# Moving the weight transposes of values and output out of the preamble of a fused attention and expert layer

## The chip, the cores and the metric

The kernel runs on one core of a Trainium2 chip. The metric is the device time of one execution in microseconds; where a kernel was run several times, the median. The engines are named as in the profile: PE (TensorE), DVE (VectorE), ACT (ScalarE), POOL (GpSimd), SP (SyncE, which here issues nearly all DMAs).

## The reference, cut to what matters

Eight batches of 512 tokens with 512 features pass a gated cross attention with 16 heads, then a mixture of 8 experts. The edit touches only the attention's beginning.

```python
def proj(x, W, b):
    return (x @ W.T + b).reshape(B, S, H, Hd).transpose(0, 2, 1, 3)
Q, K, V = proj(query, Wq, bq), proj(key, Wk, bk), proj(value, Wv, bv)   # query = layernorm(x); key = value = ctx
scores = jnp.einsum('bhqd,bhkd->bhqk', Q, K) / SCALE
attn = jax.nn.softmax(scores, axis=-1)
out = jnp.einsum('bhqk,bhkd->bhqd', attn, V)
out = out.transpose(0, 2, 1, 3).reshape(B, S, D)
x = x + jnp.tanh(g_xattn[0]) * (out @ Wo.T + bo)
x = x + jnp.tanh(g_ffn[0]) * ffn(layernorm(x))     # 8 experts, top 2, capacity limited
```

## The kernel before, in words

Each engine has one instruction list, written out by hand, and waits on semaphores. Every projection is a product of numbers split into a high and a low f16 part (three matmuls for each of four blocks of 128 features, so 12 matmuls of 128x512 a projection tile).

**Preamble.** The four weight matrices `Wq, Wk, Wv, Wo` (numbered n = 0 to 3) and the two inputs of batch 0 (`xn`, the normalised x, and `cin`, the context) have to be turned, since the contraction dimension must lie on the partitions. One *tile* is 128 features of one matrix by 512: PE writes it into a PSUM bank with 4 transposes of 128x128 f32 (`transposes`, L1207), ACT copies it out as the f16 high part (`wT[:, n, 0]`, L682, or `actT[:, n, 0]`, L677) and DVE subtracts that from PSUM for the low part (`wT[:, n, 1]`, L861, or `actT[:, n, 1]`, L853) and frees the bank. The preamble uses the four banks of `RING` (0, 1, 2, 4) in turn, so PE can be at most four tiles ahead of DVE. The order is Wq, `xn`, Wk, `cin`, Wv, Wo: 24 tiles, of which 16 are of weights. `Banks` numbers the uses of each bank; `claim` makes PE wait until all earlier uses of a bank were read, `filled` makes a reader wait for PE, `copied` waits until a use was read.

Ahead of it DVE and POOL do the layer norm of batch 0 (DVE statistics L828 and L831, POOL the inverse deviation L514 and L517, DVE the normalisation L835). PE waits first for `small_in` (biases, gates and the router's weights, six DMAs) and turns the biases; ACT does Tanh and the scaled output bias (L666 to L672) with it. At the end of the preamble DVE sets two rows of `stk` to a constant (L867, `k_ones`), and PE and SP wait until all of Wo's tiles were read.

SP issues the DMAs in this order: x of batch 0, Wq, the small inputs, Wk, context of batch 0, Wv, Wo. They land in buffers that are used for something else later: Wq and Wk in `pt`, Wv in `v32`, Wo in `xres`.

**Batch 0** (and, in a loop, the others). PE computes four of the eight projection tiles of queries and keys (`queries_keys(i)`, L1278, i = 0 to 3: q0, k0, q1, k1) and two of the four of values (`values`, L1325). ACT copies each projection twice (L715, L717), POOL subtracts (L536), SP stores it to DRAM and loads it back in the layout of the heads (`stack_heads`, L367 and L371: `stk<-qk_rows`). Then come 23 *slots*. In slot s PE computes four score blocks (`scores(s, 0..3)`, L1288, banks 0, 1, 0, 1); DVE takes the maximum of each (L874), which frees the bank. Slots 0, 1, 3 and 4 hold a further projection of queries and keys, in two halves (`filling`), slot 2 the router's transposes of `x2n` (banks 6, 7, 3, 5), slot 4 the router's products, slots 5 and 6 the other values. DVE also does one block of the layer norm of the next batch in each of the slots 1 to 4. From slot 6 on the exponentials and from slot 7 on the products with values run beside the scores.

Of the kernel before, what the change touches and what calls it, by code (L numbers as in the profile page):

```python
# [16 lines left out]
P = 128  # L17
KT = D // P
# [27 lines left out]
LN_SLOT = 1  # L46
QK_FIRST, QK_SLOT = 4, (0, 1, 3, 4)
V_FIRST, V_SLOT = 2, (5, 6)
X2T_SLOT, PARTS_SLOT, LG_SLOT = 2, 4, 5
# [11 lines left out]
def later_v(s):  # L61

    return [V_FIRST + j for j, slot in enumerate(V_SLOT) if slot == s]


# [30 lines left out]
def layer_kernel(nc, x, ctx_in, g_x, g_f, Wq, bq, Wk, bk, Wv, bv, Wo, bo, Wr, br, W1, b1, W2, b2, out):  # L96
# [9 lines left out]
    with stack:  # L106
# [113 lines left out]
        def act_banks(n):  # L220
            for kt in range(KT):
                banks.add(("actT", n, kt), RING[kt])

        banks.add("bias", 6)
        for n in range(4):
            for kt in range(KT):
                banks.add(("w", n, kt), RING[kt])
            if n < 2:
                act_banks(n)
        pre = banks.close(1)  # L230
# [160 lines left out]
        def _(sp):  # L391
# [20 lines left out]

            for kt in range(KT):
                copied(sp, pre, ("w", 3, kt))

            def store_rows(b):
# [10 lines left out]
            def batch(b, first, last):  # L427
# [11 lines left out]
                for g in range(NG):  # L439

                    sp.wait_ge(mrow_ready, NG * b + g + 1)
                    rows = stk[96:98, 0, 4 * g:4 * g + 4, :].rearrange("o h (t a q) -> o (h t) a q", t=KT, a=4)
                    for a in range(4):
                        sp.dma_start(rows[:, :, a, :], mrow[32 * a:32 * a + 32, g, :]).then_inc(mrow_in[g], 16)
                    if g == 0:
                        for i in range(QK_FIRST + 2, NQ):
                            stack_heads(sp, b, i)
                    if g == STORE_GROUP:
                        if not first:
                            store_rows(b)  # L450

                            sp.wait_ge(x1_stored, 16 * KT * b)
                            sp.wait_ge(x2n_ready, KT * b)
                        settle(sp)
                        sp.dma_start(xres[:, :, :], x_b[b]).then_inc(xres_in, 16)
# [41 lines left out]
        def _(pool):  # L497
# [165 lines left out]
        def _(act):  # L663
            s = nc.scalar
            act.wait_ge(small_in, 96)
            s.activation(tg[:, 1:2], tg[:, 0:1], ACT.Tanh).then_inc(tanh_done, 1)  # L666
            act.wait_ge(tanh_done, 1)
            s.activation(tg[:, 2:3], tg[:, 1:2], ACT.Copy, scale=1.0 / (SA * SW)).then_inc(tgbo_ready, 1)
            s.activation(tgbo[:, :], tgbo[:, :], ACT.Copy, scale=tg[:, 1:2]).then_inc(tgbo_ready, 1)
            ps, read = filled(act, pre, "bias")  # L670
            s.activation(bias[:, 0:8], ps[:, 0:8], ACT.Copy, scale=SQ).then_inc(bias_ready, 1)
            s.activation(bias[:, 8:12], ps[:, 8:12], ACT.Copy, scale=SA).then_inc(read, 1)  # L672

            def inputs_hi(n, kt):
# [3 lines left out]

            for n in range(4):
                for kt in range(KT):  # L680
                    ps, _ = filled(act, pre, ("w", n, kt))
                    s.activation(wT[:, n, 0, kt, :], ps, ACT.Copy, scale=SW).then_inc(w_hi, 1)  # L682
                if n < 2:
                    for kt in range(KT):
                        inputs_hi(n, kt)
            act.wait_ge(bias_ready, 1)
# [18 lines left out]

            def batch(b, last):
                rows, parts, logits = router_copy(use, b, b)
# [16 lines left out]
                heads_stacked(act, b)  # L724
                for i in range(QK_FIRST):
                    queries_keys(i)
                for tt in range(V_FIRST):
                    values(tt)
                for t in range(SLOTS + 1):
                    for i in later_qk(t):  # L730
                        queries_keys(i)
                    if t == X2T_SLOT:
                        rows()
# [26 lines left out]
                    if t in GROUP_NORM:  # L760
# [3 lines left out]
                                     bias=bias[:, 8 + gr:9 + gr]).then_inc(a_hi, 1)  # L764
            batch(0, False)
            with act.Fori(1, B - 1) as b:
# [54 lines left out]
        def _(dve):  # L821
# [33 lines left out]

            for n in range(4):
                for kt in range(KT):

                    dve.wait_ge(w_hi, KT * n + kt + 1)
                    ps, read = read_by_last(pre, ("w", n, kt))  # L860
                    v.scalar_tensor_tensor(wT[:, n, 1, kt, :], ps, SW, wT[:, n, 0, kt, :],  # L861
                                           ALU.mult, ALU.subtract).then_inc(read, 1)
                if n < 2:
                    for kt in range(KT):
                        inputs_split(0, n, kt)
            dve.wait_ge(tgbo_ready, 2)
            v.memset(stk[96:98, 1, :, :], SQ * SQ).then_inc(k_ones, 1)  # L867

            def batch(b, last):
                def maxima(t, qts):  # L870
# [17 lines left out]
                for t in range(SLOTS + 1):  # L888
                    maxima(t, (0, 1))
                    if t % 4 == 0 and 4 <= t <= UNITS:  # L890
# [51 lines left out]

            batch(0, False)
            with dve.Fori(1, B - 1) as b:
# [251 lines left out]
        def _(pe):  # L1196
# [27 lines left out]

            for n in range(4):
                pe.wait_ge(w_in[n], 16)
                for kt in range(KT):
                    dst, full = claim(pe, pre, ("w", n, kt))
                    transposes(dst, [raw[n][:, m, kt * P:(kt + 1) * P] for m in range(KT)]).then_inc(full, 1)
                if n < 2:  # L1230
                    for kt in range(KT):
                        inputs_transposed(0, n, kt)

            for kt in range(KT):
                copied(pe, pre, ("w", 3, kt))

# [28 lines left out]
            def batch(b, last_batch, first=False):  # L1265
# [290 lines left out]
```

## Time and profile before

| | |
|---|---|
| median of 3 runs | 1928.5 us (1927.63 to 1929.86) |
| the profiled execution's own time | 1927.96 us |
| its span | 1926.2 us |
| PE busy | 1778.0 us, 92% of the span |
| DVE busy | 1156.4 us, 60% |
| ACT busy | 778.9 us, 40% |
| POOL busy | 474.9 us, 25% |
| chain that ended last | PE 82%, DVE 10%, issue 3%, ACT 2% |

The span is the time between the first and the last record of the profile; about 1.8 us of the execution lie around it. Busy time says which engine has most to do over the whole, but the edit concerns the first 62 us alone, so the stretch matters more than the shares. All times in the rows below are microseconds from the span's start; in the timeline a row can hold several instructions ("x4"), its time then reaching from the first one's start to the last one's end, and brackets tell how long the engine was idle before it and what released it.

### The profile page before, as it was taken

How to read it: one execution, taken by the hardware profiler on the slowest of the kernel's cores; microseconds unless marked ns; L12 is line 12 of the kernel's file. 1: busy time of each engine (PE TensorE's matmuls, PEld its weight loads, DVE VectorE, ACT ScalarE, POOL GpSimd, SP SyncE). 2: the span in 40 equal slices, each digit the busy share in tenths (PEclk: the TensorE clock that was granted, in tenths of full speed). 3: DMA queues.
4: the chain of work that ended last, by engine and by line, in shares of the span. 5: the costliest groups of instructions: out<-in, count | busy, mean ns of one | idle time of the engine just before them, and what ended most of it. 6: DMA issues, size and time to landing. Idle time of an engine off the chain costs nothing.

```text
span 1926.2 us, 30517 instructions
## 1 busy us (share of the span) xinstructions
PE 1778.0 (92%) x10822; PEld 921.7 (48%) x10822; DVE 1156.4 (60%) x2163; ACT 778.9 (40%) x1012; POOL 474.9 (25%) x451
## 2 busy tenths in 40 slices
PE   7999999999999999999501999999999999999996
PEld 4334242333424333242200766666676767666664
DVE  5777777777777777867685653535353544534330
ACT  4444635445363544536310534425151615334240
POOL 2322424232242323221232111212212122112101
PEclk9999999999999999999755999999999999999998
DMA  6213232241313314032220242534343342425311
GB/s 222 90 45 110 67 126 93 76 142 44 109 66 117 101 63 135 21 108 69 89 92 27 68 140 50 162 71 136 75 122 102 100 125 74 133 63 147 73 37 25
DMA packets 138206, 178.97 MB, mean 93 GB/s; under 512 B 45493, under 2 KB 86593, under 8 KB 134057
## 3 DMA queue, kind: packets, MB, share of 16 engines
q1 hardware_dynamic: 97192, 157.85, 24.9%
q0 software_dynamic: 40960, 20.41, 6.0%
q8 instruction: 33, 0.54, 0.1%
q14 instruction: 21, 0.16, 0.0%
HBM read 134.08 MB, written 43.63 MB: 92 GB/s over the span
## 4 chain that ended last, share of the span: by engine, by line
PE 82%; DVE 10%; issue 3%; ACT 2%; POOL 1%; DMA 1%; SPq 0%; DVEq 0%; ACTq 0%; POOLq 0%
PE psum L1510 22%; PE psum L1487 20%; PE psum L1307 7%; PE psum L1314 7%; PE psum L1298 6%; PE psum L1288 5%; PE psum L1278 5%; PE psum L1400 4%; PE psum L1325 2%; DVE mx L874 2%; PE psum L1207 2%; ACT osum L759 1%; PE psum L1463 1%; DVE cmp L1024 1%; DVE x2hl L938 1%
## 5 line engine op out<-in xcount | busy, mean ns | idle before, releaser
L1510 PE MATMUL psum<-w,hT 128*123 128x512 f16 x1920 | 420.3, 379 | 0.0
L1487 PE MATMUL psum<-xgT,w 128*128 128x308 f16 (+1 forms) x3072 | 411.3, 294 | 0.6 <-DVE xgT L1133 0.6
L874 DVE TENSOR_REDUCE mx<-psum 128x1 f32<-128x512 f32 x512 | 331.1, 684 | 108.3 <-PE psum L1288 105.9
L1487 PEld LDWEIGHTS psum<-xgT,w 128*128 128x128 f16 x3072 | 298.4, 97 | 109.8 <-DVE xgT L1133 0.8
L1510 PEld LDWEIGHTS psum<-w,hT 128*123 128x123 f16 x1920 | 257.9, 135 | 148.8
L748 ACT ACTIVATE pt<-psum 128x1024 f32<-128x1024 f32 x256 | 259.1, 1021 | 166.4 <-PE psum L1298 165.8
L802 ACT ACTIVATE h<-psum,b1c 128x308 f32<-128x308 f32 (+1 forms) x256 | 117.9, 511 | 382.2 <-PE psum L1487 381.8
L1151 DVE TENSOR_TENSOR hT<-h,hT 128x615 f16<-128x615 f32 x128 | 102.6, 801 | 212.2 <-ACT hT L805 212.2
L651 POOL DMA_INDIRECT out_dram<-y,idx_now x40 | 98.9, 2472 | 499.6 <-DVE y L1186 273.9
L1278 PE MATMUL psum<-actT,wT 128*128 128x512 f16 x768 | 179.2, 381 | 2.0 <-DVE wT L861 2.0
L1288 PE MATMUL psum<-stk 96*128 96x512 f16 x512 | 171.0, 383 | 4.2 <-DVE mx L874 1.7
L786 ACT ACTIVATE w<-stage 128x2048 f16<-128x2048 f32 x64 | 121.6, 1901 | 99.2 <-DMA stage<-in_L_ffn_W_dram 99.2
L1128 DVE SCALAR_TENSOR_TENSOR w<-stage,w 128x512 f16<-128x512 f32 x240 | 156.7, 684 | 0.3 <-issue 0.3
L1298 PE MATMUL psum<-stk 98*128 98x512 f16 x512 | 153.6, 381 | 0.0
L1307 PE MATMUL psum<-pt,v 128*32 128x512 f32 x1024 | 136.4, 604 | 5.3 <-ACT osum L759 5.0
L1314 PE MATMUL psum<-pt,ones 128*32 128x512 f32 x1024 | 136.2, 604 | 0.0
L1183 DVE SCALAR_TENSOR_TENSOR y<-psum,b2b 123x512 f32<-123x512 f32 x40 | 27.7, 692 | 178.8 <-PE psum L1510 178.8
L536 POOL TENSOR_TENSOR qks<-qk,qks 128x512 f16<-128x512 f32 x64 | 75.2, 1175 | 197.4 <-ACT qks L717 143.3
L1288 PEld LDWEIGHTS psum<-stk 96*128 96x128 f16 x512 | 43.7, 98 | 166.8 <-DVE mx L874 122.9
L1278 PEld LDWEIGHTS psum<-actT,wT 128*128 128x128 f16 x768 | 75.1, 98 | 91.0 <-issue 4.4
L605 POOL DMA_INDIRECT xg<-x_split,idx_new x40 | 62.0, 1550 | 222.0 <-issue 179.0
L715 ACT ACTIVATE qk<-psum,bias 128x512 f32<-128x512 f32 x64 | 44.0, 687 | 179.0 <-PE psum L1278 173.8
(181 smaller groups left out, 1644.7 us busy)
## 6 DMA issues: line engine op xcount, KB each, us to landing
stage<-in_L_ffn_W_dram SPq DMA_DIRECT2D x64, 1024.0 KB, 5.1
stk<-qk_rows SPq DMA_DIRECT2D x192, 128.0 KB, 2.5
qk_rows<-qks SPq DMA_DIRECT2D x64, 256.0 KB, 2.5
xin<-in_x_dram SPq DMA_DIRECT2D x8, 1024.0 KB, 5.3
cin<-in_ctx_dram SPq DMA_DIRECT2D x8, 1024.0 KB, 7.5
xres<-in_x_dram SPq DMA_DIRECT2D x8, 1024.0 KB, 5.6
out_dram<-xres SPq DMA_DIRECT2D x32, 256.0 KB, 2.1
x_split<-x2hl SPq DMA_DIRECT2D x32, 256.0 KB, 2.3
```

The source lines that it names most:

```text
L748: s.activation(pt[:, (2 * u + hf) % 4, :, :], psum[:, bank:bank + 2, :], ACT.Exp, scale=1.0 / (math.sqrt(HD) * SQ * SQ)).then_inc(read, 1)
L786: s.activation(dst, stage[:, i % 2, :], ACT.Copy, scale=SW).then_inc(chunk_hi, 1)
L802: s.activation(h32[:, m % 4, c0:c1], psum[:, (2 * m + ch) % 4, 0:c1 - c0], ACT.Silu, scale=1.0 / (SX * SW), bias=b1c[:, e, m:m + 1]).then_ ...
L874: v.reduce_max(mx[:, KT * t + qt:KT * t + qt + 1], ps, AX.X).then_inc(read, 1)
L1128: v.scalar_tensor_tensor(part[1], stage[:, i % 2, cols], SW, part[0], ALU.mult, ALU.subtract).then_inc(chunk_split, 1)
L1278: last = t_.matmul(psum[:, bank, :], wT[:, n, wp, kt, m * P:(m + 1) * P], actT[:, n, xp, kt, :], start=(kt == 0 and (wp, xp) == (0, 0)), s ...
L1288: t_.matmul(dst, stk[0:96, 0, s, qt * P:(qt + 1) * P], stk[0:96, 1, s, :], start=True, stop=True).then_inc(full, 1)
L1298: last = t_.matmul(psum[:, 2 + 2 * hf + j, :], stk[0:98, 1, h, kt * P:(kt + 1) * P], stk[0:98, 0, h, :], start=True, stop=True)
L1307: t_.matmul(psum[32 * j:32 * j + 32, 6, :], v32[:, kt, HD * h:HD * h + HD], pt[:, (2 * u + j // 2) % 4, j % 2, :], start=(kt == 0), stop=( ...
L1314: last = t_.matmul(psum[32 * j:32 * j + 32, 7, :], ones32[:, :], pt[:, (2 * u + j // 2) % 4, j % 2, :], start=(kt == 0), stop=(kt == KT - 1))
L1487: mm = t_.matmul(psum[:, (2 * m + ch) % 4, 0:c1 - c0], w1[:, wp, kt, m * P:(m + 1) * P], xgT[:, xp, kt, c0:c1], start=(kt == 0 and (wp, xp ...
L1510: mm = t_.matmul(psum[0:CP, Y_BANK[c], :], hT[:, hp, k, c * CP:(c + 1) * CP], w2[:, wp, k, :], start=(k == 0 and (hp, wp) == (0, 0)), stop ...
```

## The change

The preamble keeps 16 tiles: Wq and Wk, then `xn` and `cin`. PE starts Wq without `small_in`; the bias transpose stands behind Wk, and ACT's small inputs between `xn`'s and `cin`'s tiles. Wv is turned in batch 0 between projections 1 and 2 (banks 6, 7, 3, 5), Wo in two pairs at the end of slots 0 and 1 (banks 6, 7, 6, 7). PE's wait until a matrix is read stands now ahead of its first use (for Wo ahead of the output projection), SP's wait for Wo's ahead of the load of `xres`. The memset of `stk` goes from DVE to POOL, behind the last inverse deviation of batch 0. The diff, cut to its core:

```diff
+WV_AFTER = 2
+WO_SLOT = (0, 0, 1, 1)
+def wo_tiles(s):
+    return [kt for kt, slot in enumerate(WO_SLOT) if slot == s]
...
-        banks.add("bias", 6)
-        for n in range(4):
+        for n in range(2):
             for kt in range(KT):
                 banks.add(("w", n, kt), RING[kt])
-            if n < 2:
-                act_banks(n)
+        banks.add("bias", 6)
+        for n in range(2):
+            act_banks(n)
+        for n, ring in ((2, (6, 7, 3, 5)), (3, (6, 7, 6, 7))):
+            for kt in range(KT):
+                banks.add(("w", n, kt), ring[kt])
...
 # SP: the wait moves from behind the first loads to the load of xres in batch 0
+                        else:
+                            for kt in range(KT):
+                                copied(sp, pre, ("w", 3, kt))
...
 # POOL, behind the inverse deviations of batch 0
+            pool.wait_ge(ln_rstd[0], KT)
+            g.memset(stk[96:98, 1, :, :], SQ * SQ).then_inc(k_ones, 1)
+            pool.wait_ge(k_ones, 1)
...
 # ACT
+            for n in range(2):
+                for kt in range(KT):
+                    weights_hi(n, kt)
+            for n in range(2):
+                for kt in range(KT):
+                    inputs_hi(n, kt)
+                if n == 0:
+                    small_inputs()
...
                 for i in range(QK_FIRST):
+                    if first and i == WV_AFTER:
+                        for kt in range(KT):
+                            weights_hi(2, kt)
                     queries_keys(i)
...
                     for i in later_qk(t):
                         queries_keys(i)
+                    if first:
+                        for kt in wo_tiles(t):
+                            weights_hi(3, kt)
...
 # DVE
+            for n in range(2):
+                for kt in range(KT):
+                    weights_split(n, kt)
+            for n in range(2):
+                for kt in range(KT):
+                    inputs_split(0, n, kt)
             dve.wait_ge(tgbo_ready, 2)
-            v.memset(stk[96:98, 1, :, :], SQ * SQ).then_inc(k_ones, 1)
+            for kt in range(KT):
+                weights_split(2, kt)
...
                     maxima(t, (2, 3))
+                    if first:
+                        for kt in wo_tiles(t):
+                            weights_split(3, kt)
...
 # PE
-            pe.wait_ge(small_in, 96)
-            dst, full = claim(pe, pre, "bias")
-            t_.transpose(dst[:, 0:12], bias_rows[:, :], ident[0:12, 0:12]).then_inc(full, 1)
...
+            for n in range(2):
+                for kt in range(KT):
+                    weights_transposed(n, kt)
+            pe.wait_ge(small_in, 96)
+            dst, full = claim(pe, pre, "bias")
+            t_.transpose(dst[:, 0:12], bias_rows[:, :], ident[0:12, 0:12]).then_inc(full, 1)
+            for n in range(2):
+                for kt in range(KT):
+                    inputs_transposed(0, n, kt)
...
                 for i in range(QK_FIRST):
+                    if first and i < 2:
+                        weights_copied(i)
+                    if first and i == WV_AFTER:
+                        for kt in range(KT):
+                            weights_transposed(2, kt)
                     queries_keys(i)
+                if first:
+                    weights_copied(2)
...
                     filling(s, 1)
+                    if first:
+                        for kt in wo_tiles(s):
+                            weights_transposed(3, kt)
+                if first:
+                    weights_copied(3)
```

## Rows read from the trace of the kernel before

**Rows 1.** the chain of waits, 0 to 75 us: start us, us, what

```profile
...
23.23 4.79 DVE wT L861 x8
...
28.33 12.21 PE psum L1278 x48
```

**Rows 2.** timeline of DVE and POOL, start: start us, us, engine, line, operation [idle before]

```profile
...
1.03 1.80 POOL L502 MEMSET x2n<- 128x2048 f32 x1
...
11.40 0.28 POOL L514 TENSOR_SCALAR var_eps<-mv 128x1 f32<-128x1 f32 x1 [0.45 <-DVE mv L831]
...
11.77 0.55 POOL L517 TENSOR_TENSOR rstd<-var_eps,minus_half 128x1 f32<-128x1 f32 x1
...
12.35 0.55 DVE L835 TENSOR_SCALAR xin<-xin,mv,rstd 128x512 f32<-128x512 f32 x1 [0.71 <-POOL rstd L517]
...
15.97 2.47 DVE L853 SCALAR_TENSOR_TENSOR actT<-psum,actT 128x512 f16<-128x512 f32 x4
...
18.36 2.48 DVE L861 SCALAR_TENSOR_TENSOR wT<-psum,wT 128x512 f16<-128x512 f32 x4
...
29.78 6.88 DVE L867 MEMSET stk<- 2x8192 f16 x1 [1.76 <-issue]
```

**Rows 3.** timeline of ACT, 8 to 29.9 us

```profile
...
10.73 0.20 ACT L666 ACTIVATE tg<-tg 128x1 f32<-128x1 f32 x1 [8.65 <-DMA wr<-in_L_ffn_Wr_dram]
...
11.74 0.16 ACT L672 ACTIVATE bias<-psum 128x4 f32<-128x4 f32 x1
...
17.47 2.33 ACT L682 ACTIVATE wT<-psum 128x512 f16<-128x512 f32 x4
```

**Rows 4.** timeline of PE, 9 to 33 us

```profile
...
11.03 3.68 PE L1207 MATMUL psum<-ident,pt 128*128 128x128 f32 x16
...
28.33 4.87 PE L1278 MATMUL psum<-actT,wT 128*128 128x512 f16 x14 [1.99 <-DVE wT L861]
```

**Rows 5.** instructions and transfers on the tile pt, 0 to 25 us

```profile
...
L397 SPq DMA_DIRECT2D pt<-in_L_xattn_Wq_dram x1: 492/492/492, 1.3 to 1.3; - x1
L397 SPq DMA_DIRECT2D pt<-in_L_xattn_Wk_dram x1: 548/548/548, 4.6 to 4.6; - x1
...
DMA to landing us min/median/max: 7.6/8.2/8.8
```

**Rows 6.** stretches: busy us (instructions) of PE, PEld, DVE, ACT, POOL; PE's granted clock; DMA

```profile
...
29.00:30.00 1.00, 1.00 (x4) 0.42 (x3) 0.22 (x1) 0.00 (x0) 0.00 (x0) 0.50 0.64 66
...
32.00:33.00 1.00, 1.00 (x6) 0.45 (x5) 1.00 (x1) 0.12 (x1) 0.00 (x0) 1.00 1.02 385
```

**Rows 7.** timeline of all engines, batch 0's first slots

```profile
...
41.59 1.25 SPq L371 DMA_DIRECT2D stk<-qk_rows  x3
...
45.55 0.60 PE L1288 MATMUL psum<-stk 96*128 96x512 f16 x2
...
52.37 0.68 DVE L828 BATCH_NORM_STATS2 stats<-xin 128x6 f32<-128x512 f32 x1
52.48 0.60 PE L1288 MATMUL psum<-stk 96*128 96x512 f16 x2
...
53.30 2.45 DVE L874 TENSOR_REDUCE mx<-psum 128x1 f32<-128x512 f32 x4
...
54.84 1.04 PE L1207 MATMUL psum<-ident,x2n 128*128 128x128 f32 x8
...
59.85 0.60 PE L1288 MATMUL psum<-stk 96*128 96x512 f16 x2
```

**Rows 8.** the page's DMA issues: name, count, KB each, median us to landing

```profile
...
stk<-qk_rows SPq DMA_DIRECT2D x192, 128.0 KB, 2.5
```

**Rows 9.** timeline, POOL and DVE at the end of batch 0

```profile
...
153.39 1.15 POOL L536 TENSOR_TENSOR qks<-qk,qks 128x512 f16<-128x512 f32 x1
...
153.46 1.37 DVE L835 TENSOR_SCALAR x2n<-xres,mv,rstd 128x512 f32<-128x512 f32 x1 [0.45 <-POOL rstd L517]
...
```

**Rows 10.** ACT's table loads in the groups by line

```profile
...
L666 ACT ACT_TABLE_LOAD x1 | 1.3, 1283 | 0.8 <-PEq L1546 0.8
```

More of the change, by code:

```diff
@@ L411, in _ @@
             sp.dma_start(tgf[:, 0:1], g_f.rearrange("(a e) -> a e", a=1).to_broadcast((P, 1))).then_inc(r_in, 16)
-            for kt in range(KT):
-                copied(sp, pre, ("w", 3, kt))
             def store_rows(b):
@@ L664, in _ @@
             s = nc.scalar
[L665 to L672, printed above, removed]
             def inputs_hi(n, kt):
@@ L677, in inputs_hi, with weights_hi, small_inputs @@
                 s.activation(actT[:, n, 0, kt, :], ps, ACT.Copy, scale=(1.0, SX)[n]).then_inc(act_hi, 1)
-            for n in range(4):
-                for kt in range(KT):
[L681 to L685, printed above, removed]
+            def weights_hi(n, kt):
+                ps, _ = filled(act, pre, ("w", n, kt))
+                s.activation(wT[:, n, 0, kt, :], ps, ACT.Copy, scale=SW).then_inc(w_hi, 1)
+            def small_inputs():
+                act.wait_ge(small_in, 96)
+                s.activation(tg[:, 1:2], tg[:, 0:1], ACT.Tanh).then_inc(tanh_done, 1)
+                act.wait_ge(tanh_done, 1)
+                s.activation(tg[:, 2:3], tg[:, 1:2], ACT.Copy, scale=1.0 / (SA * SW)).then_inc(tgbo_ready, 1)
+                s.activation(tgbo[:, :], tgbo[:, :], ACT.Copy, scale=tg[:, 1:2]).then_inc(tgbo_ready, 1)
+                ps, read = filled(act, pre, "bias")
+                s.activation(bias[:, 0:8], ps[:, 0:8], ACT.Copy, scale=SQ).then_inc(bias_ready, 1)
+                s.activation(bias[:, 8:12], ps[:, 8:12], ACT.Copy, scale=SA).then_inc(read, 1)
+            for n in range(2):
+                for kt in range(KT):
+                    weights_hi(n, kt)
[4 more added lines that the diff above has]
+                    small_inputs()
             act.wait_ge(bias_ready, 1)
@@ L704, in router_copy, with batch @@
                 return rows, parts, logits
-            def batch(b, last):
+            def batch(b, last, first=False):
                 rows, parts, logits = router_copy(use, b, b)
@@ L764, in batch @@
                                      bias=bias[:, 8 + gr:9 + gr]).then_inc(a_hi, 1)
-            batch(0, False)
+            batch(0, False, True)
             with act.Fori(1, B - 1) as b:
@@ L854, in inputs_split, with weights_split, batch @@
                                        ALU.mult, ALU.subtract).then_inc(read, 1)
-            for n in range(4):
-                for kt in range(KT):
[L859 to L865, printed above, removed]
+            def weights_split(n, kt):
+                dve.wait_ge(w_hi, KT * n + kt + 1)
+                ps, read = read_by_last(pre, ("w", n, kt))
+                v.scalar_tensor_tensor(wT[:, n, 1, kt, :], ps, SW, wT[:, n, 0, kt, :],
+                                       ALU.mult, ALU.subtract).then_inc(read, 1)
+            for n in range(2):
+                for kt in range(KT):
+                    weights_split(n, kt)
+            for n in range(2):
+                for kt in range(KT):
+                    inputs_split(0, n, kt)
             dve.wait_ge(tgbo_ready, 2)
-            v.memset(stk[96:98, 1, :, :], SQ * SQ).then_inc(k_ones, 1)
-            def batch(b, last):
+            for kt in range(KT):
+                weights_split(2, kt)
+            def batch(b, last, first=False):
                 def maxima(t, qts):
@@ L941, in batch @@
                                     ALU.subtract).then_inc(x2hl_ready, 1)
-            batch(0, False)
+            batch(0, False, True)
             with dve.Fori(1, B - 1) as b:
@@ L1223, in inputs_transposed, with weights_transposed, weights_copied @@
                 transposes(dst, [(xn, cin)[n][:, tt, kt * P:(kt + 1) * P] for tt in range(KT)]).then_inc(full, 1)
-            for n in range(4):
-                pe.wait_ge(w_in[n], 16)
-                for kt in range(KT):
[L1228 to L1235, printed above, removed]
+            def weights_transposed(n, kt):
+                if kt == 0:
+                    pe.wait_ge(w_in[n], 16)
+                dst, full = claim(pe, pre, ("w", n, kt))
+                transposes(dst, [raw[n][:, m, kt * P:(kt + 1) * P] for m in range(KT)]).then_inc(full, 1)
+            def weights_copied(n):
+                for kt in range(KT):
+                    copied(pe, pre, ("w", n, kt))
+            for n in range(2):
[7 more added lines that the diff above has]
+                    inputs_transposed(0, n, kt)
             def router(where, b, n):
```

## Prediction

> **What bounds the kernel now.** I read the page's first part for the busiest engine: PE, 92% of the span (the table above). The edit touches only the stretch from the start to about 62 us, so I then read the chain of waits in order of time there. The reader is to see three pieces: until 10.7 us everything waits for the last small input (the router's weights, through `small_in`) [rows 3]; until 28.02 us the chain runs on DVE, which makes the second halves of 24 tiles; from 28.33 us it is PE's own matmuls [rows 1]. The timelines of DVE, ACT and PE show how [rows 2 to 4]: every tile is turned by PE, copied by ACT, subtracted by DVE, in a ring of four banks, and DVE is the slowest at 0.60 us a tile (four take 2.39 us from one group's start to the next's, 15.97 to 18.36 us). After batch 0's first score the chain passes between PE and DVE for some 13 us [rows 7]; later PE has no long wait until the attention ends. So a shift of PE at slot 4 of batch 0 goes to the end unchanged. That is where I make the sum: what PE starts at 59.85 us before [rows 7], when does it start after?
>
> **1. Earlier start of the projections: gain.** Before, DVE does 24 tiles before the first projection. After, it does 8 of weights and 8 of inputs, and PE's first projection needs bank 2, whose last user is tile 15 (`actT`, 1, kt 2). DVE cannot start before its last normalisation ends, 12.35 + 0.55 = 12.90 us [rows 2]; nothing in the edit shortens that. Wq lands at 1.3 + 7.6 = 8.9 us, Wk at 4.6 + 8.8 = 13.4 us [rows 5]. PE need no longer wait for `small_in`, so it turns Wq's 16 pieces at the first group's slow pace, 3.68 us [rows 4], from 8.9 to 12.6 us, and all four tiles lie ready when DVE comes. DVE reads tile 1 by 13.6 us, which frees the bank for Wk, landed by then. At 0.60 us a tile, tile 13 would start at 12.90 + 7.2 = 20.1 us.
>
> Between tiles 12 and 13 ACT has now the small inputs: from 10.73 to 11.90 us before, some 1.17 us [rows 3]. ACT runs 18.36 - 17.47 = 0.89 us ahead of DVE and its copy takes 0.6, so 0.3 us of it is covered: DVE stalls 0.85 us, tile 13 starts at 20.95, tile 15 ends at 20.95 + 1.2 + 0.68 = 22.83. The step from DVE to PE was 0.3 us (28.02 to 28.33), so the first projection starts at 23.15 us: **5.2 us earlier**. PE idles 2.2 us before it (its last transpose ends near 20.9), as it did 1.99 us before [rows 4]; there the granted clock fell to 0.50, 1.2 GHz, until about 32 us [rows 6]. The last of the first 14 matmuls begins 4.5 us after the first [rows 4]; at the 0.216 us of the later ones (34 in the rest of 12.21 us [rows 1]) it would be 2.8: 1.7 us lost, in both kernels, and I let it cancel. Not falling would gain up to 1.7 us.
>
> **2. Wv's transposes between projections 1 and 2: loss.** 16 of them on PE, with nothing to hide them, and their four banks are free. Eight take 1.0 us where PE is not held by DVE (54.84 us) [rows 7]: **+2.0 us**. ACT copies the four tiles in 2.3 us and DVE's parts end about 1 us after it, some 5 us before values 0 asks for them, so ACT and DVE cost nothing here. If that cover were gone, values 0 would wait for them, at most the 2.4 us of four tiles.
>
> **3. The stacking through DRAM.** SP's chain of stores and loads moves with the first projection, and projection 2's delay of 2.0 us hides behind SP, which was still busy with projection 1. The first scores' last operand is loaded from 41.59 us, 13.3 us after the first projection [rows 7]; after: 36.4 plus 1.3 of issue plus 2.5 of landing [rows 8], 40.2 us. PE comes for it at 45.55 - 5.2 + 2.0 = 42.4 us. Covered by 2 us. SP asks for batch 1's inputs at ACT's last input tile, again just ahead of the first projection, so their transfers meet the same part of the work. SP's wait for Wo's tiles moves to the load of `xres`, behind the second group's maxima; by then slot 1 is long over, and it costs nothing.
>
> **4. Wo's transposes in slots 0 and 1: loss on PE, and a new wait.** Again 16: **+2.0 us** on PE. But each pair stands behind a projection's second half. In slot 0 projection 4 ends at 45.9 us, the pair at 46.9. ACT first makes its two copies of the projection (1.2 us, from 46.1), then the two weight tiles: ready at 47.9 and 48.5. DVE subtracts at 47.95 and 48.55, and by the program's order its maxima of slot 1 stand behind them: the first ends at 49.85. Meanwhile PE has put scores 0 and 1 of slot 1 and half of projection 5 (1.3 us) by 48.65 and needs bank 0 for score 2: it waits 1.2 us, and 0.4 more for bank 1. Slot 1 with its pair ends at 53.0. Before, the two slots took 6.93 us (45.55 to 52.48) [rows 7]; after, 10.6.
>
> In slot 2 the router's transposes need bank 6, which now holds Wo's tile 2: ACT reaches it at 53.4, DVE frees it at 54.73; PE waits 1.3 us. DVE then does its layer norm row (0.93 us, 52.37 to 53.30 before [rows 7]) and only then the slot's maxima, at 56.25, for which PE waits 1.0 and 0.4 us. Slot 2 ends at 58.7. In slot 3 DVE still trails: PE waits 0.3 us, where it had waited 0.6. Slot 4 starts at 62.5 against 59.85 us: **+2.65 us**. The same as a sum: -5.2 + 2.0 + 2.0 + 3.85 of waits that slots 1 to 3 had not before.
>
> **5. The memset of `stk` from DVE to POOL.** On DVE it took 6.88 us in time nobody waited for [rows 2]. POOL wrote 2048 values per partition in 1.80 us [rows 2], so 8192 take about 7.2 us, bounds 6.9 (DVE's) to 7.4: from 12.4 to 19.8 us. POOL's next work is the first projection's lower half near 28.8; PE asks for it at 42.4. Its cost is nothing as long as DVE is not held by it. That is not sure: at the end of batch 0 POOL starts a subtraction at 153.39 us for 1.15 us, and DVE's normalisation, which starts at 153.46, takes 1.37 instead of 0.55 us [rows 9]. POOL's memset becomes ready with the same semaphore as DVE's last normalisation. Before, DVE started 0.03 us after it (12.32 to 12.35), and POOL's own step, which waits for POOL's step before it, 0.09 us (11.68 to 11.77) [rows 2]. So I take it that DVE comes first.
>
> The Trainium skill ("SBUF — State Buffer", section "Who interferes with whom") states this as a rule: DVE's two-port instructions and any GpSimd instruction take one pair of ports for the whole instruction, and the first to start wins. Rows 9 agree. By that rule with POOL first the last normalisation would stand behind the whole memset.
>
> **6. The table.** One table load, 1.28 us, stands ahead of Tanh [rows 10]. Now a Copy is ACT's first function. Were another set loaded for it, Tanh would bring a second load into the stretch of step 1, where every 1.28 us counts. Before, Copy, Tanh and Exp run under one load, so I take nothing; the bound is +1.28 us. The Trainium skill ("ScalarE activation tables: per-element evaluation and per-set limits", section "Table sets in the compiler and the runtime") says that loads are placed by the longest run that one set serves, which also gives no second load.
>
> **The sum.** The profiled execution took 1927.96 us (span 1926.2). 1927.96 + 2.65 = 1930.6; the median of the runs is 0.54 higher than the profiled one, so I forecast **1931.1 us**, 0.14% above the median before.
>
> **The rivals.** What can be told from no change here is about 0.2%, 3.9 us.
> - *A, as summed*, 1931.1 us, its own range 1930 to 1932.3: chance 0.44.
> - *B, PE's clock costs more.* Two places: Wk's 16 transposes may still be slow after PE's idle microsecond (0.86 instead of 0.60 us a tile: up to +0.8), and the waits of 1.2 to 1.3 us in slots 1 and 2, each shorter than the 1.99 us after which the clock fell, may lower it, at up to +1.7 each. For it: in slot 2 PE would be idle half of the time. 1931.9 to 1935.3; over 1932.4 it is slower by more than 0.2%. Chance 0.26.
> - *C, less is lost*: the clock does not fall before the first projection (-1.7), or ACT's and DVE's queues clear so that the 3.85 us of waits are not there. Floor: -5.2 + 4.0 - 1.7, 2.9 us under before, 1925.6. With one of them: 1927.3 to 1929.4. Chance 0.17.
> - *D, the memset holds DVE* (step 5), the rival on the other side: it decides if POOL starts before DVE, a margin of 0.06 us. The last normalisation ends near 19.9 instead of 12.9, everything behind it shifts by 7.0 us: 1938.1. Chance 0.08.
> - *E, a second table load*: 1931.1 + 1.28 = 1932.4. Chance 0.05.
>
> **Range and chances.** 1927.6 to 1935 leaves D out and the tail of C. Slower by over 0.2%: D, half of E, most of B and the upper edge of A, 0.37. Faster by over 0.2% would need more than C's floor, 0.04. Within 0.2%: 0.59.
>
> **What the changed profile would show.** The first matmul of the projections near 23.2 us after DVE's tile 15; small inputs near 19 us on ACT with DVE idle about 0.9 us behind them; 16 transposes of about 2.0 us between projections 1 and 2; the first score near 42.4 us; PE waiting for DVE's maxima in slot 1, for bank 6 in slot 2; slot 4 near 62.5 us. Wrong would be: a normalisation of 7 us on DVE (D), a table load near 19 us (E), a granted clock of 0.50 between 47 and 60 us (B) or of 1.00 at 24 us (C).

## The result, and the profile after

| | before | after |
|---|---|---|
| median of 5 runs | 1927.97 us (1927.24 to 1929.86) | 1938.98 us (1938.25 to 1940.24) |
| ratio of the runs | | 1.0057, 95% interval 1.0042 to 1.0071 |
| profiled execution, its span | 1927.96 us, 1926.2 us | 1940.14 us, 1938.3 us |
| PE, DVE, POOL busy | 1778.0, 1156.4, 474.9 us | 1780.6, 1156.9, 482.0 us |

The kernel is slower by 11.0 us in the medians, outside the predicted range, and close to rival D's 1938.1 us. The busy times say nothing of it: no engine has 11 us more work. The timeline of all engines from the start has the larger part of it in its second and third line here.

```profile
...
9.23 3.38 PE L1241 MATMUL psum<-ident,pt 128*128 128x128 f32 x16 [9.23 <-DMA pt<-in_L_xattn_Wq_dram]
...
12.48 7.23 DVE L862 TENSOR_SCALAR xin<-xin,mv,rstd 128x512 f32<-128x512 f32 x1 [0.71 <-POOL rstd L527]
12.50 6.92 POOL L533 MEMSET stk<- 2x8192 f16 x1
...
19.63 3.26 DVE L887 SCALAR_TENSOR_TENSOR wT<-psum,wT 128x512 f16<-128x512 f32 x5
...
20.44 3.65 PE L1241 MATMUL psum<-ident,pt 128*128 128x128 f32 x16 [7.83 <-DVE wT L887]
...
27.58 0.21 ACT L691 ACTIVATE tg<-tg 128x1 f32<-128x1 f32 x1
...
29.29 2.48 DVE L880 SCALAR_TENSOR_TENSOR actT<-psum,actT 128x512 f16<-128x512 f32 x4 [0.64 <-ACT actT L681]
...
31.32 5.34 PE L1319 MATMUL psum<-actT,wT 128*128 128x512 f16 x24 [1.96 <-DVE actT L880]
```

DVE's last normalisation, 0.55 us before [rows 2], takes 7.23 us. POOL's memset of `stk` is recorded from 12.50 to 19.42 us, and the normalisation ends 0.29 us after it. It starts 0.02 us *ahead* of the memset and is held all the same. DVE's splits begin at 19.63 instead of 12.81, so PE, which had Wq turned at 12.6 us as predicted, stands until 20.44 for the first bank. Wk's 16 transposes then take 3.65 us at a granted clock of 0.50 (the stretch 20 to 24 us), against 2.36 us in k2 below. The small inputs on ACT hold DVE up for 0.64 us. The first projection starts at 31.32 us, 3.0 us later than before [rows 4] where 5.2 us earlier was forecast.

The chain of waits agrees: DVE's one instruction is the largest piece ahead of the projections, and in slots 0 to 2 the chain goes to DVE's splits of Wo.

```profile
...
12.48 7.23 DVE xin L862
...
20.44 3.65 PE psum L1241 x16
...
36.66 1.75 PE psum L1241 x16
...
54.11 1.29 DVE wT L887 x2
55.40 1.21 DVE mx L905 x2
...
60.22 1.29 DVE wT L887 x2
```

PE's timeline in batch 0's slots, to be held against [rows 7]:

```profile
...
48.60 0.60 PE L1329 MATMUL psum<-stk 96*128 96x512 f16 x2
...
56.05 0.39 PE L1329 MATMUL psum<-stk 96*128 96x512 f16 x1 [1.22 <-DVE mx L905]
...
56.65 0.39 PE L1329 MATMUL psum<-stk 96*128 96x512 f16 x1 [0.21 <-DVE mx L905]
...
61.06 1.16 PE L1241 MATMUL psum<-ident,x2n 128*128 128x128 f32 x8 [1.41 <-DVE wT L887]
...
63.07 0.39 PE L1329 MATMUL psum<-stk 96*128 96x512 f16 x1 [0.85 <-DVE mx L905]
...
64.07 1.91 PE L1241 MATMUL psum<-ident,x2n 128*128 128x128 f32 x8
...
69.76 0.60 PE L1329 MATMUL psum<-stk 96*128 96x512 f16 x2
```

The first score stands at 48.60 us (45.55 before), slot 4 at 69.76 (59.85 before). PE waits for DVE's maxima in slot 1 (1.22 and 0.21 us), for bank 6 in slot 2 (1.41), then again for maxima (0.85 and 0.21). And in slot 2 the second eight transposes of `x2n` take 1.91 instead of 1.04 us. The stretches say why, and the first of them shows the same for Wk's transposes (busy us and instructions of PE, PEld, DVE, ACT, POOL, then PE's granted clock):

```profile
...
core 0: us, PE busy (x) PEld busy (x) DVE busy (x) ACT busy (x) POOL busy (x), PEclk, DMA share, GB/s
...
22.00:24.00 2.00, 2.00 (x10) 1.69 (x8) 1.57 (x4) 1.36 (x3) 0.00 (x0) 0.50 0.00 0
...
31.00:34.00 3.00, 2.68 (x13) 1.29 (x14) 0.77 (x2) 0.00 (x0) 0.00 (x0) 1.00 0.66 209
...
61.00:64.00 3.00, 1.88 (x10) 1.19 (x11) 2.85 (x6) 1.13 (x2) 0.00 (x0) 0.90 0.26 87
64.00:66.00 2.00, 2.00 (x10) 1.79 (x9) 1.69 (x4) 0.60 (x1) 0.00 (x0) 0.50 0.68 197
```

After the waits of slots 1 and 2 the clock falls to 0.50, that is 1.2 GHz, until the beginning of slot 3. On the other hand it had not fallen at the first projections, though PE had idled 1.96 us there.

At slot 4 the changed kernel is 9.9 us behind. Of the 12.2 us between the two profiled executions the other 2.3 arise later, in parts the edit doesn't touch. The largest piece, 1.5 us, stands behind the routing of the tokens, where PE takes up work again at 1057.83 us before and at 1068.43 us after: from there to SP's second set of expert weights (at 1082.67 and 1094.75 us) it is 24.84 and 26.32 us. What differs there is how long PE's clock stays at 0.50; two rows are shown with the second run of k2 below. Differences of this size also stand between runs of one kernel: the 33 runs of the kernel before beside the second set of experiments spread from 1924.3 to 1930.7 us.

### The profile page after: what moved, and what is told of

Its sections match the earlier page's. It is cut to its first block, busy times and chain, and to the rows that moved or that the text cites. A ratio compares the mean times of both kernels' runs of the same rounds, so it can differ in the third digit from the quotient of the medians.

```text
span 1938.3 us, 30547 instructions
## 1 busy us (share of the span) xinstructions
PE 1780.6 (92%) x10822; PEld 925.0 (48%) x10822; DVE 1156.9 (60%) x2162; ACT 778.5 (40%) x1012; POOL 482.0 (25%) x452
## 4 chain that ended last, share of the span: by engine, by line
PE 83%; DVE 10%; ACT 3%; issue 2%; POOL 1%; DMA 1%; DVEq 0%; ACTq 0%; POOLq 0%
PE psum L1563 21%; PE psum L1540 20%; PE psum L1348 7%; PE psum L1355 7%; PE psum L1339 6%; PE psum L1319 6%; PE psum L1329 5%; PE psum L1453 4%; PE psum L1366 3%; PE psum L1241 2%; DVE mx L905 2%; ACT osum L786 1%; PE psum L1516 1%; DVE cmp L1058 1%; DVE cnt L1063 1%
```

## The experiments

Nine kernels were run, one of them twice. All but k3 start from the changed kernel. This table takes from each profiled execution when the first projection, the first score and slot 4 start on PE, and whether the granted clock fell to 0.50 at the first projection (P) or in slot 2 (S); medians and ratios are those of the repeated runs against the kernel before on the same chip (its medians there: 1927.66 us beside k1 to k4, 1928.41 beside k5 to k7 and k2 again, 1927.89 beside k8 and k10).

| kernel | projection | score | slot 4 | clock fell | profiled | median | ratio, interval |
|---|---|---|---|---|---|---|---|
| before | 28.33 | 45.55 | 59.85 | P | 1927.96 | 1927.97 | |
| changed | 31.32 | 48.60 | 69.76 | S | 1940.14 | 1938.98 | 1.0057, 1.0042 to 1.0071 |
| k1 memset on DVE | 24.23 | 44.41 | 65.58 | P, S | 1935.14 | 1933.88 | 1.0030, 1.0018 to 1.0042 |
| k2 memset waits | 22.79 | 41.76 | 62.05 | P | 1929.37 | 1933.58 | 1.0031, 1.0019 to 1.0043 |
| k2 again | 22.69 | 39.97 | 60.25 | none | 1928.76 | 1930.35 | 1.0013, 1.0003 to 1.0022 |
| k3 memset alone | 35.33 | 51.17 | 65.47 | none | 1933.71 | 1935.31 | 1.0039, 1.0025 to 1.0053 |
| k4 in 16 pieces | 22.98 | 41.95 | 62.25 | P | 1931.17 | 1932.46 | 1.0028, 1.0016 to 1.0039 |
| k8 memset 0.2 us later | 22.95 | 41.92 | 63.22 | P, S | 1933.74 | 1931.30 | 1.0017, 1.0007 to 1.0026 |
| k5 Wo ahead of the slots | 22.69 | 43.41 | 57.69 | P | 1926.28 | 1926.26 | 0.9989, 0.9980 to 0.9998 |
| k7 Wo first in its slot | 22.73 | 41.70 | 58.14 | P | 1926.84 | 1927.39 | 0.9995, 0.9986 to 1.0005 |
| k6 Wv in PE's gap | 24.08 | 41.36 | 55.64 | none | 1923.87 | 1923.87 | 0.9979, 0.9970 to 0.9988 |
| k10 small inputs last | 24.47 | 41.75 | 56.03 | none | 1920.73 | 1926.22 | 0.9994, 0.9985 to 1.0003 |

Two things that the table doesn't separate have to be kept in mind when two of its profiles are compared. Wk's 16 transposes took 3.65 us in the profiles of the changed kernel, k1 and k6 and 2.33 to 2.36 us in the others that begin their preamble in the same way, which makes the first projection some 1.4 us later (24.23 us in k1, 22.79 in k2). In the changed kernel the granted clock was 0.50 there; in k1 and k6 the profile has 1.00 beside the same 3.65 us, so why they were slow there is open. And from slot 4 to the end of the span the profiles take between 1865.6 and 1868.8 us, k10's alone 1863.0.

### The memset: k1, k2, k3, k4, k8

**k1** puts the memset back on DVE:

```diff
-            pool.wait_ge(ln_rstd[0], KT)
-            g.memset(stk[96:98, 1, :, :], SQ * SQ).then_inc(k_ones, 1)
-            pool.wait_ge(k_ones, 1)
...
             for kt in range(KT):
                 weights_split(2, kt)
+            v.memset(stk[96:98, 1, :, :], SQ * SQ).then_inc(k_ones, 1)
```

> The changed kernel with the memset of stk back on DVE, behind its splits of Wv. Theory P (POOL's memset holds DVE's last normalisation of batch 0 for its whole length): the normalisation takes 0.55 us again, the first projection starts near 24 us instead of 31.3, and the time falls by some 7 us, to 1931 to 1932.5 us. Rival Q (the memset is harmless, the loss lies in batch 0's slots and in a clock that falls): the time stays near 1938 to 1939 us.

Measured: 1933.88 us, 5.1 us under the changed kernel's median. The normalisation takes 0.55 us and the first projection starts at 24.23 us. It is above the expected 1932.5. Two lines of PE's timeline show two parts of what is missing to the 7 us, held against the changed kernel: the clock falls at the first projections, whose 24 matmuls take 7.03 instead of 5.34 us, and the first score waits.

```profile
...
24.23 7.03 PE L1317 MATMUL psum<-actT,wT 128*128 128x512 f16 x24 [1.85 <-DVE actT L877]
...
44.41 0.60 PE L1327 MATMUL psum<-stk 96*128 96x512 f16 x2 [1.04 <-DVE stk L896]
```

It waits 1.04 us for DVE's memset, which now starts only behind Wv's splits (37.47 us) and ends at 44.35: moved back naively, it is late. So the first projection is 7.1 us earlier than in the changed kernel, but the first score and slot 4 are only 4.2 us earlier. Against the expectation two things more count: Wk's slow transposes, and the clock, which fell in slot 2 in this profile too, as it had in the changed kernel's.

**k2** leaves the memset on POOL but starts it when DVE's normalisation is done:

```diff
-            pool.wait_ge(ln_rstd[0], KT)
+            pool.wait_ge(xn_ready, KT)
```

> The changed kernel with the memset still on POOL, but begun only when DVE's last normalisation is done (it waits for xn_ready). It then runs beside DVE's splits, which read PSUM and one SBUF tile. Theory P, with the hold at instructions that go from SBUF to SBUF: the splits keep their pitch of 0.60 us and the time is that of the memset on DVE, 1931 to 1932.5 us. Rival: any DVE instruction is held by POOL's memset; then the first split takes 7 us and the time stays near 1939 us.

```profile
...
12.48 0.55 DVE L862 TENSOR_SCALAR xin<-xin,mv,rstd 128x512 f32<-128x512 f32 x1 [0.72 <-POOL rstd L527]
...
13.09 6.92 POOL L533 MEMSET stk<- 2x8192 f16 x1 [0.64 <-DVE xin L862]
...
56.83 0.39 PE L1329 MATMUL psum<-stk 96*128 96x512 f16 x1 [0.21 <-DVE mx L905]
...
57.05 1.04 PE L1241 MATMUL psum<-ident,x2n 128*128 128x128 f32 x8
```

The normalisation takes 0.55 us, and the memset beside DVE's splits costs these nothing: eight splits from 12.86 us take 4.87 us, 0.60 each, in the second profile. So POOL's memset holds the normalisation (SBUF to SBUF) and not the splits (PSUM and one SBUF tile to SBUF). Slot 4 starts at 62.05 us; the forecast had 62.5. The median, though, is 1933.6 us in the first set and 1930.4 in the second, on either side of the expected 1931 to 1932.5, against a profiled 1929.37; that is taken up with the second profile, below.

**k3** is the kernel before with the memset's move alone (the same three lines behind the inverse deviations, DVE's memset taken out).

> The kernel before with this one edit: the memset of stk goes from DVE to POOL, behind the last inverse deviation. Theory P: DVE's last normalisation takes 7.2 instead of 0.55 us; the first weights' tiles then lie ready (the four of Wq come 0.6 instead of 0.86 us apart, which gives some 0.7 us back), so the first projection starts about 6 us later and the time is 1934 us, 6 us over before. Rival Q: no change, 1928 us.

```profile
...
12.47 7.23 DVE L838 TENSOR_SCALAR xin<-xin,mv,rstd 128x512 f32<-128x512 f32 x1 [0.72 <-POOL rstd L517]
12.50 6.92 POOL L523 MEMSET stk<- 2x8192 f16 x1
...
35.33 10.52 PE L1280 MATMUL psum<-actT,wT 128*128 128x512 f16 x48 [1.99 <-DVE wT L864]
```

Ratio 1.0039, some 7.5 us: this edit by itself makes the kernel slower. The first projection is 7.0 us later (35.33 against 28.33). The expected return of 0.7 us did not come: PE idled 6.2 us and then turned `xn`'s 16 pieces in 3.65 us at a granted clock of 0.50. In this profile another return did: the clock stayed at 1.00 at the projections, whose 48 matmuls take 10.52 instead of 12.21 us, so slot 4 is 5.6 us later than before and the profiled time 5.75 us higher. The five runs lie in two groups, two near 1933.6 us (the profiled one among them) and three from 1935.3 to 1935.7; that in the upper ones the clock fell at the projections fits the 1.7 us between them, but is not shown.

**k4** cuts the memset into 16 of 512 columns (`for h in range(H): g.memset(stk[96:98, 1, h, :], ...)`).

> The changed kernel with POOL's memset cut into 16 of 512 columns each, about 0.45 us apiece. If the hold lasts as long as POOL's one instruction, DVE's last normalisation waits for one or two pieces: 1.0 to 1.5 us instead of 7.2, and the time is 1932 to 1933.5 us. If POOL kept DVE out for as long as it has memsets queued, the normalisation would still take about 7 us and the time stays near 1939 us.

```profile
...
12.41 0.83 DVE L863 TENSOR_SCALAR xin<-xin,mv,rstd 128x512 f32<-128x512 f32 x1 [0.72 <-POOL rstd L527]
12.44 7.81 POOL L534 MEMSET stk<- 2x512 f16 x16
```

The normalisation takes 0.83 us, 0.3 more than alone and less than the 1.0 to 1.5 expected: by its length it waits out one piece and gets in between two. The hold is that of one POOL instruction, whatever is queued behind. The time, 1932.46 us, is in the expected range.

**k8** puts a memset of one column, and a wait for it, ahead of the long one, so that it starts later by a little.

```diff
             pool.wait_ge(ln_rstd[0], KT)
+            g.memset(pause[:, 0:1], 0.0).then_inc(k_ones, 1)
+            pool.wait_ge(k_ones, 1)
             g.memset(stk[96:98, 1, :, :], SQ * SQ).then_inc(k_ones, 1)
-            pool.wait_ge(k_ones, 1)
+            pool.wait_ge(k_ones, 2)
```

> The changed kernel with one memset of a single column on POOL, and a wait for it, ahead of the memset of stk: the long memset then starts some 0.2 us later than DVE's last normalisation, which takes 0.5 us, instead of 0.02 us later. Theory W (the one that has really begun first keeps the other out, and 0.02 us between the recorded starts was not enough of a lead for DVE): the normalisation takes 0.55 to 0.7 us, the memset ends a little later, the time is that of the kernel in which it waits, near 1931 us. Rival: POOL's memset takes over even from a running DVE instruction; then the normalisation still takes 7 us and the time stays near 1939 us.

```profile
...
12.66 0.55 DVE L865 TENSOR_SCALAR xin<-xin,mv,rstd 128x512 f32<-128x512 f32 x1 [0.71 <-POOL rstd L528]
12.69 0.10 POOL L534 MEMSET pause<- 128x1 f32 x1
...
12.84 7.23 POOL L536 MEMSET stk<- 2x8192 f16 x1
```

Now the long memset is recorded 0.18 us behind the normalisation, and it is the memset that is held, 7.23 instead of 6.92 us; DVE keeps its 0.55. The same two instructions with 0.02 to 0.03 us between their starts went the other way. So, as far as one profile tells, the first to begin does keep the other out, as theory W has it, but at 0.03 us the order of the recorded starts does not tell which that is. The time falls to 1931.3 us with 0.16 us more distance between the two starts.

### The slots and the clock: k5, k7, k2 again

**k5** takes k2 and turns Wo's four tiles between projections 2 and 3 (banks 6, 7, 3, 5) instead of in slots 0 and 1:

```diff
-WO_SLOT = (0, 0, 1, 1)
+WO_SLOT = ()
...
+                    if first and i == 3:
+                        for kt in range(KT):
+                            weights_transposed(3, kt)
```

> The changed kernel with POOL's memset begun behind DVE's last normalisation, and all four tiles of Wo turned between projections 2 and 3 instead of in slots 0 and 1. Theory S (PE waits in slots 1 and 2 for DVE, whose splits stand behind ACT's copies of the projection, and PE's clock falls in those waits): no wait of PE for maxima in slot 1 and none for bank 6 in slot 2, the same 2.0 us of transposes, slot 4 begins near 58.2 us instead of 62.05, and the time is 1926 to 1927.5 us, some 4 us or more under that kernel with Wo in the slots. Rival T (only PE's 4 us of transposes count, the waits in the slots stand in for waits that were there before): slot 4 near 62 us and no change of the time.

Slot 4 starts at 57.69 us, 4.4 us earlier than in k2, with the same transposes on PE. The time is 1926.26 us, its 11 runs stay within 3.4 us, and the interval of its ratio ends at 0.9998, just under the kernel before.

**k7** keeps the pairs in the slots and only changes the order: on PE `weights_transposed(3, kt)` ahead of `filling(s, 1)`, on ACT `weights_hi(3, kt)` ahead of `queries_keys(i)`.

> The changed kernel with the memset begun behind the last normalisation, and in slots 0 and 1 Wo's pair turned ahead of the projection's second half (on ACT its copies ahead of the projection's). PE has the same work in the same slots; only the order behind which DVE's splits stand is another. Theory S: the waits in slots 1 and 2 go, slot 4 near 58.3 us, the time within 1 us of that with Wo ahead of the slots. Rival T: the slots are too full for DVE's 2.4 us more, whatever the order: slot 4 near 62 us.

Starts of slots 1 and 2, the wait for the maximum in slot 2, and slot 4, in PE's timeline:

```profile
...
46.03 0.60 PE L1329 MATMUL psum<-stk 96*128 96x512 f16 x2
...
50.37 0.60 PE L1329 MATMUL psum<-stk 96*128 96x512 f16 x2
...
52.32 0.39 PE L1329 MATMUL psum<-stk 96*128 96x512 f16 x1 [0.48 <-DVE mx L905]
...
58.14 0.60 PE L1329 MATMUL psum<-stk 96*128 96x512 f16 x2
```

Slots 0 and 1 take 4.33 and 4.34 us, which is 3.47 for a slot before plus 0.87 for a pair. No wait in slot 1; one of 0.48 us in slot 2. With the same work in the same slots, the order in PE's and ACT's lists was worth 3.9 us at slot 4 (62.05 to 58.14). The expectation of a time within 1 us of k5's was missed by 0.1 us.

**k2 again**, for a second profile.

> The changed kernel with the memset begun behind the last normalisation, once more beside these three, for a second profile: its median was 1933.6 us, its first profiled execution 1929.37 us. If the difference is PE's clock in slot 2, this profile or the spread of the times shows it: a granted clock of 0.50 for some 2.5 us behind PE's waits in slot 2, and slot 4 near 64 us.

The second profile does not show the fall in slot 2. But the 10 runs lie in two heaps, five from 1928.8 to 1929.2 and five from 1931.5 to 1934.5 us, both profiles of k2 belong to the lower one, and k8, the same work in the same places, was profiled in its upper one (1933.74 us) with the clock fallen in slot 2. The clock's mean over the whole run is on record for each of the 10: 0.965 to 0.966 in the lower heap, 0.962 to 0.964 in the upper one. So the heaps differ by PE's clock, though this doesn't say where it was low. Six profiles hold the long waits of slots 1 and 2 (the changed kernel, k1, k2 twice, k4, k8); in three of them the clock fell there. In k5, k6 and k7, where no wait of the slots reaches half a microsecond, no profile shows such a fall.

From the lower profile of k2 to that of k8 there are 5.0 us, of which 3.0 have arisen by slot 4 (60.25 to 63.22), where the clock fell twice in k8 and not at all in k2. The other 2.0 have nearly all arisen where PE takes up work again behind the routing, between there and SP's second set of expert weights: 24.70 us in k2, 26.61 in k8. PE's first transposes there, and a stretch about 7 to 9 us (k2) and 6 to 8 us (k8) behind their start, with PE's granted clock:

```profile
...
1058.74 4.81 PE L1516 MATMUL psum<-ident,xg 123*128 123x123 f16 x40 [16.50 <-DMA xg<-x_split,idx_new]
...
1066.00:1068.00 2.00, 2.00 (x17) 1.47 (x16) 2.00 (x14) 0.36 (x1) 0.00 (x0) 1.00 0.00 0
```

```profile
...
1061.79 5.05 PE L1519 MATMUL psum<-ident,xg 123*128 123x123 f16 x40 [16.37 <-DMA xg<-x_split,idx_new]
...
1068.00:1070.00 2.00, 2.00 (x10) 1.14 (x9) 2.00 (x10) 0.00 (x0) 0.00 (x0) 0.50 0.00 0
```

Ten matmuls in 2 us at 0.50 against 17 at 1.00: the clock, near 0.50 in both kernels all through the routing, is back before 1064 us in k2 and only after 1070 in k8. So some 2 us of the difference between these two profiles have nothing to do with the first slots. Which of the unprofiled runs lost how much in which place stays open.

What the two profiles of k2 differ in is the first projections, whose 24 matmuls (two projections) take 7.03 us in one and 5.34 in the other, behind the same idle time:

```profile
...
22.79 7.03 PE L1319 MATMUL psum<-actT,wT 128*128 128x512 f16 x24 [1.87 <-DVE actT L880]
```

```profile
...
22.69 5.34 PE L1319 MATMUL psum<-actT,wT 128*128 128x512 f16 x24 [1.86 <-DVE actT L880]
```

This makes slot 4 1.8 us later in the first one; from the last store of `x_split` to the second set of expert weights it then needs 138.60 instead of 139.83 us, so the times differ by only 0.6 us.

### Towards a better order: k6, k10

**k6** takes k2 and moves Wv's transposes ahead of projection 0, into the time in which PE waits for DVE, and Wo's between projections 1 and 2.

> Memset begun behind the last normalisation, Wv's transposes ahead of projection 0, in PE's idle 1.9 us before it, Wo's four tiles between projections 1 and 2. Expected: Wv's transposes cost no time, since PE waits there for DVE's tile 15 anyway, and PE's clock need not fall to 0.50 before the projections. Slot 4 begins near 56.3 us if the clock falls all the same and near 54.7 us if it does not, against 59.85 before; the time is 1923 to 1925 us, under both kernels. If ACT's and DVE's work on Wv delays the projections' copies, the gain is less than 1 us over the kernel with Wo ahead of the slots.

```profile
...
22.05 2.48 DVE L882 SCALAR_TENSOR_TENSOR actT<-psum,actT 128x512 f16<-128x512 f32 x4 [0.53 <-ACT actT L681]
22.07 1.91 PE L1245 MATMUL psum<-ident,v 128*128 128x128 f32 x16
...
24.08 5.34 PE L1323 MATMUL psum<-actT,wT 128*128 128x512 f16 x24
```

Wv's transposes run from 22.07 us beside DVE's last four splits of the context, and the projections follow 0.1 us behind them at full clock. This execution had Wk's transposes at the slow pace (3.65 us), so the first projection is at 24.08 us and slot 4 at 55.64, between the two expected values; that is all the same 4.2 us ahead of the kernel before. Median 1923.87 us over 11 runs, ratio 0.9979 with an interval up to 0.9988: the fastest version, 0.2% under the kernel before.

**k10** is k6 with the small inputs behind the context's tiles on ACT (`if n == 1: small_inputs()`).

> The kernel with Wv ahead of projection 0 and Wo between projections 1 and 2, and ACT's small inputs behind the context's tiles instead of between those of x and of the context. If the small inputs hold DVE up there (0.53 us of idle time before tile 13), tile 13 starts about 0.6 us earlier and so does the first projection if DVE is what it waits for; but PE's 16 transposes of Wv end only just before it, so less than 0.6 us may come through: the time is 0 to 0.6 us under that kernel's 1923.9 us, too little to be told from no change by the times, and to be read from the start of slot 4 (55.64 us there).

```profile
...
22.39 0.16 ACT L697 ACTIVATE bias<-psum 128x4 f32<-128x4 f32 x1
...
22.69 1.94 PE L1245 MATMUL psum<-ident,v 128*128 128x128 f32 x16 [1.84 <-ACT bias L697]
```

The expectation missed a wait. The bias transpose and Wv's first tile share bank 6, and ACT now reads the bias at 22.39 us, so Wv's transposes stand 1.84 us idle for it and the first projection starts at 24.47 us, later than in k6. The median is 1926.2 us, 2.3 us over k6's, where 0 to 0.6 us less was expected. At slot 4 only 0.4 us is lost in the profile, but the two profiles aren't alike: k6's had Wk's transposes slow (3.65 us) and k10's had them fast (2.33 us), so k10's order costs more than 0.4 us; an estimate from these numbers is 0.4 + 1.3 = 1.7 us. That this wait makes most of the median's 2.3 us is likely and not shown. The profiled execution is also by far the fastest of k10's 11 runs (1920.73 us, the next 1925.64): behind slot 4 it needed 3.5 us less than k6's, in the stretch of the routing. Its time says nothing for k10.

## Why the prediction was wrong

**The step that failed** is step 5, "Its cost is nothing as long as DVE is not held by it ... So I take it that DVE comes first." It had found the mechanism, its price and the row that shows it, and then decided a race between two engines by a lead of 0.06 us in recorded starts, giving the other outcome 0.08. The changed profile shows DVE recorded 0.02 us ahead and held for 7.2 us; k3 shows the price alone (7.0 us at the first projection, 7.5 in the medians), k2 that 0.6 us of delay on POOL takes it away, k8 that 0.16 us is enough. The price of the hold was right: 7.0 forecast, 7.0 at k3's first projection. That the whole time forecast for this case, 1938.1 us, comes so close to 1938.98 is in part luck: against k2 the changed kernel's first projection is 8.5 us later, since PE stood and then turned Wk and `xn` at 0.50; the clock that didn't fall at the first projections gave 1.7 back, the one that fell in slot 2 took 0.9, and this leaves 7.7 at slot 4. Terms that the forecast for this case did not hold have nearly cancelled. The Trainium skill's rule ("SBUF — State Buffer", section "Who interferes with whom") is borne out by k4, k8 and k2: one holder for one whole instruction, and no contention for DVE's splits, which have one SBUF input.

**Steps that held**, by k2, where the hold is away:
- Step 1: the first projection at 22.7 to 22.8 us, forecast 23.15. The small inputs cost DVE 0.54 us, forecast 0.85.
- Step 2: Wv's transposes 1.75 us on the chain of waits, forecast 2.0.
- Step 3: no first score waited for the stacking through DRAM in any of the profiles with Wv's tiles moved.
- Step 4: a pair of Wo 0.87 us, forecast 1.0; waits of 1.22 and 0.21 us in slot 1 (1.2 and 0.4), 1.42 for bank 6 (1.3), 0.85 and 0.21 for maxima (1.0 and 0.4). Slot 4 at 62.05 us, forecast 62.5. k7 confirms the cause: DVE's splits stood behind ACT's copies of the projection. In k2's second profile slot 4 is at 60.25 us, since the clock did not fall at the first projections (rival C).
- Step 6: one table load ahead of the first tile and none at Tanh. The only other one stands at the experts' activation in both kernels (1066.86 us before, 1078.95 after).
- The sum: 0.54 us were added for the distance of the median from the profiled time, and these came from three runs; with five runs the median before is 1927.97 us, the profiled time itself.

**A second term stood at nothing in the sum**: the clock in the slots, rival B, priced there at up to 1.7 us each. The changed kernel, k1 and k8 show it at 0.50 in slots 2 and 3 in their profiles. Before `x2n`'s second half k1 and k2 ran alike; from the first score to slot 4 k1 took 21.17 us and k2 20.29, and the changed kernel 21.16: 0.9 us for the fall. The runs of k2 spread over 5.7 us where k5's spread over 3.4. So even without the hold the changed order measures 1.0013 to 1.0031, some 2.5 to 6 us, over the kernel before, where 2.65 was forecast; the upper end isn't explained by 0.9 us. k8's profile shows a second place, up to 1.9 us behind the routing, which the prediction did not look at and the edit doesn't touch. B's other term, Wk's transposes at up to 0.8 us, measured 1.4 us at the first projection where it came (k1 against k2).

**Rival C** was right in one half: the clock need not fall before the first projection. In the changed kernel that gave back about 1.7 us, which Wv's transposes (1.75 us) took again before the first score.

## What to carry to other kernels

Where an engine's work moves to POOL, look at which of DVE's SBUF-to-SBUF instructions become ready by the same semaphore; a lead of a few hundredths of a microsecond in the recorded starts decides nothing, and one wait more, or cutting the long instruction into pieces, removes the risk for next to nothing. Work that is moved out of a stage bound by one engine isn't free on the engine that bounds the next stage: it pays best in a gap of that engine (k6), and a helper engine's jobs on which another engine's queue hangs belong ahead of its others in the same slot (k7). A short wait on PE costs more than its length where it lets the clock fall, and it may do so in one execution and not in the next; so a profile should be compared with the spread of the runs before its time is believed (k10).

## What the runs showed of the hardware

- A POOL memset that only writes 2 partitions (6.92 us) holds a DVE instruction of 128 partitions from SBUF to SBUF for its whole length (7.23 us), even where DVE's recorded start is 0.02 to 0.03 us earlier; with DVE 0.18 us ahead it is POOL that is held (7.23 instead of 6.92 us).
- The same kernel with the same idle time of 1.86 us on PE had the granted clock at 0.50 behind it in one execution and at 1.00 in another (k2's two profiles, 7.03 and 5.34 us for 24 matmuls). Idle times of 1.99 us went one way each too: 0.50 in the kernel before (48 matmuls in 12.21 us), 1.00 in k3 (10.52 us).
- Behind the routing, during which the granted clock is near 0.50 throughout, it was back at 1.00 some 4.5 us after PE had taken up work in k2's second profile and some 9 us after it in k8's and the changed kernel's.
